# An attention stage in which scores and attention products stand together, and keys are transposed two sequences ahead

## What is computed

```python
q = query + braak_embed[braak_stages][..., None]
attn = softmax(einsum('bsd,btd->bst', q, key))          # key = value = side
o = einsum('bst,btd->bsd', attn, value)
nx = o * rsqrt(mean(o * o) + EPS) * norm_w
weights = top_2_of(softmax(nx @ gate_w.T))              # of 8 experts
h1, h3 = base1 + SCALING * (nx @ a1.T) @ b1.T, base3 + SCALING * (nx @ a3.T) @ b3.T
out = x + sum_e weights_e * ((silu(h1) * h3) @ (w2.T + SCALING * a2.T @ b2.T))
```

## Time and profile before

| | |
|---|---|
| median of 3 runs | 1300.16 us (1297.99 to 1302.87) |
| the profiled execution | 1298.83 us, its span 1297.0 us |
| TensorE busy, share of the span | 1290.4 us, 99% |
| VectorE | 856.6 us, 66% |
| ScalarE | 531.4 us, 41% |
| GpSimd | 232.0 us, 18% |

### The profile page before, as it was taken

One profiled execution on the slowest core, in us unless ns is written; L12 is line 12 of the kernel. 1 busy time (PEld: TensorE's weight loads), 2 busy tenths in 40 slices (PEclk: granted clock), 3 DMA queues, 4 the chain that ended last, 5 costly groups with the idle time before them and its releaser, 6 DMA issues.

```text
span 1297.0 us, 18613 instructions
## 1 busy us (share of the span) xinstructions
PE 1290.4 (99%) x7190; PEld 1128.4 (87%) x7190; DVE 856.6 (66%) x1582; ACT 531.4 (41%) x991; POOL 232.0 (18%) x189
## 2 busy tenths in 40 slices
PE   9999999999999999999999999999999999999998
PEld 8999988888888888888888888888888888888887
DVE  6898756656675666756765666566665676575656
ACT  6877744334333334333432333333433333333332
POOL 3444530202020200202020202020110202020200
PEclk9999999999999999999999999999999999999999
DMA  9777630010202020101011020202020101102000
GB/s 285 163 170 175 172 95 4 28 48 1 74 2 73 1 71 4 59 16 46 28 30 46 1 74 2 73 1 74 2 63 12 54 20 40 36 3 71 1 17 17
DMA packets 116419, 69.73 MB, mean 54 GB/s; under 512 B 57694, under 2 KB 107372, under 8 KB 116204
## 3 DMA queue, kind: packets, MB, share of 16 engines
q1 hardware_dynamic: 116020, 68.54, 19.2%
q10 hardware_dynamic: 312, 0.02, 0.0%
HBM read 51.40 MB, written 17.14 MB: 53 GB/s over the span
## 4 chain that ended last, share of the span: by engine, by line
PE 99%; ACT 0%; DVE 0%; issue 0%; DVEq 0%
PE bank L1295 31%; PE bank L1294 31%; PE bank L1296 31%; PE bank L1421 2%; PE bank L1347 1%; PE bank L1399 1%; PE bank L1340 0%; PE bank L1306 0%; ACT prob L739 0%; ACT qT_hi L722 0%; DVE neg_max L968 0%; DVE x_out L1238 0%; PE bank L1386 0%; PE bank L1314 0%; ACT kT_hi L723 0%
## 5 line engine op out<-in xcount | busy, mean ns | idle before, releaser
L1166 DVE TENSOR_TENSOR act_a<-silu_a,bank 128x512 f32<-128x512 f32 x128 | 87.7, 685 | 211.7 <-PE bank L1296 195.1
L830 ACT ACTIVATE br_hi<-act_br 128x512 fp32r<-128x512 f32 x128 | 80.9, 632 | 187.9 <-DVE act_br L1177 187.9
L823 ACT ACTIVATE silu_b<-bank 128x512 f32<-128x512 f32 x128 | 76.3, 596 | 187.9 <-PE bank L1296 187.1
L1295 PE MATMUL bank<-w2T_lo,s_hi 128*128 128x256 f32 x512 | 144.7, 283 | 0.0
L1296 PE MATMUL bank<-w2T_hi,s_lo 128*128 128x256 f32 x512 | 143.3, 280 | 0.0
L1294 PE MATMUL bank<-w2T_hi,s_hi 128*128 128x256 f32 x512 | 142.7, 279 | 0.0
L1174 DVE TENSOR_TENSOR act_b<-silu_b,bank 128x512 f32<-128x512 f32 x128 | 88.0, 687 | 81.0 <-PE bank L1296 80.1
L660 POOL TENSOR_TENSOR t_lo<-t_in,t_hi 128x512 fp32r<-128x512 f32 x32 | 40.6, 1290 | 552.2 <-ACT t_hi L810 552.2
L819 ACT ACTIVATE silu_a<-bank 128x512 f32<-128x512 f32 x128 | 75.8, 592 | 134.7 <-PE bank L1296 134.6
L679 POOL TENSOR_TENSOR v_lo<-v_full,v_hi 128x512 fp32r<-128x512 f32 x64 | 94.5, 1509 | 136.7 <-ACT v_hi L815 136.7
L1187 DVE TENSOR_TENSOR br_lo<-act_br,br_hi 128x512 fp32r<-128x512 f32 x128 | 104.7, 818 | 5.6 <-ACT br_hi L830 3.1
(11 more groups left out here) (201 smaller groups left out, 3213.4 us busy)
## 6 DMA issues: line engine op xcount, KB each, us to landing
kv<-in_fside_BxSxS SPq DMA_DIRECT2D x32, 256.0 KB, 3.2
t_scratch<-oT SPq DMA_DIRECT2D x32, 256.0 KB, 2.6
t_in<-t_scratch SPq DMA_DIRECT2D x32, 256.0 KB
out<-x_out SPq DMA_DIRECT2D x52, 128.0 KB
x_in<-in_x SPq DMA_DIRECT2D x96, 64.0 KB, 2.7
x_out<-in_x SPq DMA_DIRECT2D x48, 128.0 KB
rho<-scale_scratch SPq DMA_DIRECT2D x16, 256.0 KB
rstd<-scale_scratch SPq DMA_DIRECT2D x16, 256.0 KB
```

Source lines behind the costliest of these rows:

```text
L823: nc.scalar.activation(silu_b[:, :], h1_bank[j % 2][:, :], ACT.Silu).then_inc(silu_b_ready, 1)
L830: nc.scalar.activation(br_hi[j % 2][:, :], act_br[j % 2][:, :], ACT.Copy).then_inc(br_hi_ready, 1)
L1166: nc.vector.tensor_tensor(act_a[j % 2][:, :], silu_a[j % 2][:, :], h3_bank[j % 2][:, :], ALU.mult).then_inc(act_a_ready, 1)
L1295: nc.tensor.matmul(dst, w_hi, x_lo, start=False, stop=False, skip_group_check=not grouped)
```

## The change

From step 10 on (`PAIRED`), TensorE and ScalarE call a `paired_step`. On TensorE it is: `scores(c)`, `attend(c - 1)`, the query transposes of c + 1 where there are any, the key transposes of **c + 2**, the first half of the gate of c - 2, `transpose_prob(c)`, the second half of the gate. Step 10 has the key transposes of both 11 and 12. On ScalarE it is: values, queries of c + 1, exponentials, copy of the attention output, probabilities, keys of c + 2. The joint semaphores for queries and keys are taken apart (`qT_ready`, `kT_ready`, `qT_lo_ready`, `kT_lo_ready`), and the key transposes of c wait until the low part of the keys of c - 1 has been taken, `kT_lo_ready` at c. For VectorE a `paired_step` is defined too, but nothing calls it: its loop is not in the diff. SyncE is unchanged, GpSimd but for the names of its semaphores.

```diff
@@ ScalarE
+            def k_high(c):
+                act.wait_ge(kT_ready, c + 1)
                 nc.scalar.activation(kT[c % 2][0][:, :], kT_bank[:, :], ACT.Copy).then_inc(kT_hi_ready, 1)
...
+            def paired_step(c):
+                value_high(c)
+                if c + 1 in TURNED:
+                    q_high(c + 1)
+                if c == PAIRED[0]:
+                    k_high(c + 1)
+                exp(c)
+                copy_oT(c - 1)
+                if c + 1 < BATCH and c + 1 not in TURNED:
+                    q_high(c + 1)
+                probT_high(c)
+                if c + 2 < BATCH:
+                    k_high(c + 2)
...
-            for c in range(ROWS_STEP):
+            for c in range(PAIRED[0]):
                 step(c, c in JOB_STEPS)
+            for c in range(PAIRED[0], ROWS_STEP):
+                paired_step(c)
                 if c == ROUTE_STEP + 8:
                     exp_gap(0)
...
             for c in range(ROWS_STEP, BATCH):
-                step(c)
-                if c - 1 in T0_STEPS:
-                    first_t_high(c - 1 - T0_STEPS[0])
+                paired_step(c)
+                if c - 2 in T0_STEPS:
+                    first_t_high(c - 2 - T0_STEPS[0])
@@ VectorE
+            def k_low(c):
                 dve.wait_ge(kT_hi_ready, c + 1)
                 nc.vector.tensor_tensor(kT[c % 2][1][:, :], kT_bank[:, :], f32(kT[c % 2][0][:, :]), ALU.subtract
-                                        ).then_inc(qkT_lo_ready, 1)
+                                        ).then_inc(kT_lo_ready, 1)
...
@@ in step(c), which the loop over all sequences calls
                 if c + 1 < BATCH:
-                    qk_low(c + 1)
+                    q_low(c + 1)
+                    k_low(c + 1)
...
+            def paired_step(c):
+                row_max(c)
+                if c + 1 < BATCH:
+                    k_low(c + 1)
+                if c + 1 in TURNED:
+                    q_low(c + 1)
+                beside(c - 1)
+                if c + 2 in TURNED:
+                    turn_q(c + 2)
+                if c + 1 < BATCH and c + 1 not in TURNED:
+                    q_low(c + 1)
+                keep_gate(c - 2)
+                probT_low(c)
@@ TensorE
+            def transpose_q(c):
+                pe.wait_ge(q_ready, c + 1)
+                transpose_seq(q[c % 2], qT_bank).then_inc(qT_ready, 1)
+
+            def transpose_k(c):
                 pe.wait_ge(kv_loaded[c % RING], 16 * (c // RING + 1))
-                transpose_seq(kv[c % RING], kT_bank).then_inc(qkT_ready, 1)
+                pe.wait_ge(kT_lo_ready, c)
+                transpose_seq(kv[c % RING], kT_bank).then_inc(kT_ready, 1)
...
             def scores(c):
-                pe.wait_ge(qkT_lo_ready, c + 1)
+                pe.wait_ge(qT_lo_ready, c + 1)
+                pe.wait_ge(kT_lo_ready, c + 1)
...
+            def paired_step(c):
+                scores(c)
+                if c == PAIRED[0]:
+                    transpose_k(c + 1)
+                attend(c - 1)
+                if c + 1 < BATCH and c + 1 not in TURNED:
+                    transpose_q(c + 1)
+                if PAIRED[0] < c and c + 2 < BATCH:
+                    transpose_k(c + 2)
+                wait_gate(c - 2)
+                gate_half(c - 2, 0)
+                transpose_prob(c)
+                gate_half(c - 2, 1)
+                if c == PAIRED[0]:
+                    transpose_k(c + 2)
...
-            for c in range(ROWS_STEP):
+            for c in range(PAIRED[0]):
                 step(c, c in JOB_STEPS)
+            for c in range(PAIRED[0], ROWS_STEP):
+                paired_step(c)
             pe.wait_ge(w_lo_ready, JOBS)
             transpose_rows(0, row_bank)
             for c in range(ROWS_STEP, BATCH):
-                step(c)
+                paired_step(c)
```

More of the change, by code:

```diff
@@ L366, in turned_no, with plain_no @@
             return c - TURNED[0] + 1
+        def plain_no(c):
+            return sum(k not in TURNED for k in range(c + 1))
         def mixed(c):
@@ L387, in group_in @@
             return c // 2 + 1
+        PAIRED = range(ROUTE_STEP, BATCH)
         ROUTE_TILES = range(0, TILES - 2, 2)
@@ L633, in add_bias @@
                 if c - 2 in TURNED:
-                    pool.wait_ge(qkT_lo_ready, c - 1)
+                    pool.wait_ge(qT_lo_ready, c - 1)
+                else:
+                    pool.wait_ge(qT_ready, plain_no(c - 2))
                 pool.wait_ge(q_ready, c)
-                pool.wait_ge(qkT_ready, c - 1)
                 pool.wait_ge(xs_loaded[c % RING], xs_count(c))
@@ L1365, in first_transpose_qk @@
                                                    q[0][:, h, dc * P:(dc + 1) * P], ident[:, :])
-                last.then_inc(qkT_ready, 1)
+                last.then_inc(qT_ready, 1)
             def scores(c):
-                pe.wait_ge(qkT_lo_ready, c + 1)
+                pe.wait_ge(qT_lo_ready, c + 1)
+                pe.wait_ge(kT_lo_ready, c + 1)
                 for h in range(SC):
@@ L1411, in attend, with gate_half, wait_gate @@
                 last.then_inc(o_ready, 1)
-            def gate(c, first=False):
+            def gate_half(c, h):
+                for dc in range(DC):
+                    last = nc.tensor.matmul(gate_bank[:, h * GATE_STRIDE:(h + 1) * GATE_STRIDE],
+                                            oT[c % 2][:, dc, h, 0:P], oT[c % 2][:, dc, h, 0:GATE.stop],
+                                            start=(dc == 0), stop=(dc == DC - 1))
+                if h == SC - 1:
+                    last.then_inc(gate_ready, 1)
+            def wait_gate(c, first=False):
                 if first:
@@ L1418, in gate @@
                 pe.wait_ge(oT_copied, c + 1)
+            def gate(c, first=False):
+                wait_gate(c, first)
                 for h in range(SC):
-                    for dc in range(DC):
-                        last = nc.tensor.matmul(gate_bank[:, h * GATE_STRIDE:(h + 1) * GATE_STRIDE],
-                                                oT[c % 2][:, dc, h, 0:P], oT[c % 2][:, dc, h, 0:GATE.stop],
-                                                start=(dc == 0), stop=(dc == DC - 1))
-                last.then_inc(gate_ready, 1)
+                    gate_half(c, h)
             def transpose_rows(r, dst):
@@ L1444, in step @@
                 if c + 1 < BATCH:
-                    transpose_qk(c + 1)
+                    if c + 1 not in TURNED:
+                        transpose_q(c + 1)
+                    transpose_k(c + 1)
                 if jobs_here:
```

42 lines of the change are left out of this document (23 added, 19 removed).

## The result

| | before | changed |
|---|---|---|
| median | 1299.08 us (1297.03 to 1302.87, 6 runs) | 1338.76 us (1336.37 to 1341.09, 6 runs) |
| ratio to before, 95% interval | | 1.0304 [1.0291, 1.0316] |
| the profiled execution | 1298.83 us, span 1297.0 | 1339.66 us, span 1337.9 |
| attention stage from sequence 10 on | 104.11 us | 144.87 us |

What follows compares the result with a forecast made beforehand. TensorE was taken as the bound, VectorE next. Step 10 5.05, nine routing steps 63.9, eight plain 46.0, routing rows 0.2, last four 24.2: 139.4 against 104.1, +35.3 us, forecast 1334.5; range 1331 to 1338 (0.60), whole range 1324 to 1345.

Steps and rivals of the forecast that it cites:

- VectorE in the new order: Rival: VectorE's loop was misread; wait of 0.22 us in 18 steps, +4 to +6, 1304; 0.04 together with no slowdown.
- A plain step, 5.75 us: Attention steps 19 and 21 to 27, without routing piece: 5.75 us each against 4.64, together 46.0.
- In a plain step the queries' low part gets in at once: VectorE asks at 2.64 us, gets in at 2.78 behind GpSimd's values' low part, ends at 3.33 as without GpSimd.
- in every step: Rival: GpSimd's bias sum comes first in steps without routing piece too, making them 6.75 us; +8, 1342.5; chance 0.20.
- A routing step, 7.1 us: Nine attention steps with a routing piece (11 to 18 and 20): 7.1 us each, together 63.9.
- nine full holds at 7.45: Case where small routing instructions are held by GpSimd like large ones: 7.45 us a step, sum 38 instead of 35.
- My middle of two cases: In steps with a routing piece, 7.1 us taken between 7.45 (small instructions held by GpSimd) and 6.75 (not held).
- GpSimd never costs: 1329: Rival: the nine steps with a routing piece take 5.75 us plus their piece, together 58.8; +30 us, 1329; chance 0.15.
- Step 10 and the last four: Attention step 10, with two key transposes, 5.05 us; steps 28 to 31 together 24.2, against 20.16 before.
- Not slower: Rival: keys' low part in time, needing VectorE 1.15 us earlier; some 1297; 0.04 together with VectorE's order being misread.
- Fewer changes between plain and split products: TensorE's 24 products in one row instead of two: at most 0.02 us a step, 0.4 over 22 steps, taken as nothing.
- The signs: Foretold: 5.7 to 5.8 us in sequences 21 to 27, two TensorE waits, VectorE nearly never idle, expert stage unchanged.

Runs made afterwards that it cites:

- the run with the fillers: The changed kernel with nine unread fp32 products of 128 columns added on TensorE in each of steps 11 and 18; 1338.31 us, ratio 1.0296.

## Why the prediction was right, and where it was off

- **VectorE still runs the old order.** Shown by the edit to its loop: 33 of 39.7 us. The rival "VectorE in the new order" was put at 1304 with a wait of 0.22 us a step; the kernel that calls it took 1305.56, with steps 4.88 against 4.64.
- **A plain step, 5.75 us.** Measured 5.82. The chain came out link by link: start of the block transposition forecast at 0.78, seen at 0.81; attention products 2.15, seen 2.23; maximum 2.02, seen 2.01; queries' low part 2.64, seen 2.60; key transposes 3.98, seen 4.09; remainder 1.77, seen 1.74. Its 0.06 for getting going again is an estimate that no row shows by itself, nor does a run.
- **In a plain step the queries' low part gets in at once.** Right in seven of eight: 0.73 us, and it was the bias sum that took 1.50 instead of 1.06. The rival "in every step" fell by that. In step 19 the bias sum came first (132.78 against 132.97), and the queries' low part took 1.42. But what I took as a matter of this one turn is a fixed point: as the kernel with the gate copies last shows, a VectorE that comes 0.3 us earlier is held 0.3 us longer.
- **A routing step, 7.1 us.** The term of the sum that was too small: nine took 67.89 us instead of 63.9, past even the 67 of nine full holds at 7.45. Without a fall of the clock the steps 11 and 18 take 7.74 and 7.52 us, as the run with the fillers shows; with these the nine are 65.9, 7.32 each, between my 7.1 and the 7.45 of the full hold. The mechanism was wrong too. I had the queries' low part meet the bias sum. In all nine steps it runs free, at 0.68 or 0.69 us, and a small instruction ahead of it is held as a large one would be (0.95 for 0.17, 0.74 for 0.22). The Trainium skill (SBUF — State Buffer, Who interferes with whom) has it so, whatever the size, and adds that a tensor_scalar can be held too; the 0.51 us of `g_logits` against 0.18 agrees. In this kernel that hold moved more than it added: the piece waits out the bias sum, and the queries' low part behind it then has nothing to wait for. My middle of two cases was no mechanism; that the steps 13, 14 and 20 came out at 7.10 to 7.12 is luck.
- **Nothing was said of the clock.** The other 2 us of the nine, and 0.7 of step 19, are the two falls. No stretch of the stage before showed one, and I did not ask what a TensorE that waits up to 2.5 us in a step would be granted.
- **GpSimd never costs: 1329.** The rival was priced rightly, but GpSimd does cost: only with it held back does the kernel take 1329.16, and the nine routing steps 58.6 against the 58.8 of its sum.
- **Step 10 and the last four.** 5.07 and 24.32 us, forecast 5.05 and 24.2; step 29 7.64, forecast 7.6.
- **Not slower.** I priced it at 1297 and gave "VectorE 1.15 us earlier" as its condition. The kernel that reaches 1298.6 has four things, of which I had named one: VectorE's order, the gate's first half ahead of the key transposes on TensorE (0.25 us a plain step), GpSimd's bias sum elsewhere, and the loads of keys ahead of the masks.
- **Fewer changes between plain and split products.** Taken as nothing, and nothing it was: with every wait covered, a step is 4.62 to 4.65 against 4.64.
- **The signs.** Plain steps of 5.81 to 5.83 us, two waits of TensorE in each (0.56 and 0.20 in the brackets, shorter than forecast) and an expert stage of its old length came as named. Two signs did not: VectorE is not nearly without idle time, it sits idle 2.18 of 5.82 us, as my own chain has it (done at 3.93, next due 0.28 into the next step), and the low part of the queries is not over 1 us long in the routing steps.

The sum was 35.3 us, the stage grew by 40.8: 4.0 in the routing steps, 0.9 in step 19 (0.7 of it the clock) and 0.5 in the plain ones lie above it, the rest below 0.2 each.

## What to carry to other kernels

When one engine's order is rewritten, read the order of every engine that it waits for: here two engines moved and the third kept a loop that called its old function, and the cost was over six times what both orders together cost. Price a changed step as one chain across engines from the step's start, and ask of each link which other engine it must take turns with, since a link that comes earlier may only wait longer (the gate copies were worth nothing until GpSimd's instruction was moved). Work of GpSimd on SBUF belongs beside VectorE instructions that read PSUM, and whatever is needed one step sooner must also be loaded one step sooner in a queue that runs in order.

## What the hardware showed that I had not expected

- The granted clock fell behind single waits of TensorE of 1.90 to 2.76 us, but not behind each of them: a wait of 1.90 us was followed by a fall (step 18 of the changed kernel), one of 1.92 in its step 15 by none, nor one of 2.17 in step 29 of the kernel with the routing piece behind the keys, nor one of 2.93 in step 11 of the kernel with the gate copies last. What decides between them stays open. The Trainium skill (TensorE: Matmul & The Clock Gate, HAM oscillation — how this bites in real kernels) describes a clock that falls again and again while TensorE waits for loads; here it fell once or twice in a stage, behind waits for VectorE.
- A fall cost 0.7 us (step 11) and 2.0 (steps 18 and 19), and the changed kernel's runs of 1336.4 to 1341.1 us line up with their mean granted clock, 0.999 to 0.996. Spread by itself is no sign of it: the kernel with the gate copies last and GpSimd held back shows a fall in its profile, and its four runs lie within 0.6 us; the one with VectorE's new order shows none, and its four lie 2.9 apart.
- Port holds go both ways: beside the queries' low part the bias sum took 1.50 us instead of 1.06. Who is held is decided by who came first: 0.3 us earlier, in the kernel with the gate copies last, the queries' low part is held too, by the values' low part (1.04 us), and the bias sum behind it again takes 1.52.
